# New places for a step's side work, an earlier head of the expert stage, and three of the last step's products with C on VectorE

## What is computed

```python
h = einsum('bhid,oi,od->bho', x, weighted_sum, weight)
x = layernorm(h)
for _ in range(4):
    xr = rmsnorm(x) @ W_in;  x_in, res = split(xr, 2)
    u = silu(causal_conv4(x_in) + conv_b)
    dt, Bm, Cm = split(u @ W_x)                       # 64, 16, 16
    delta = softplus(dt @ W_dt + b_dt)
    # for each of 16 states s, along the 512 tokens:
    h_s[t] = exp(delta[t] * A[s]) * h_s[t-1] + delta[t] * u[t] * Bm[t, s]
    y[t] = sum_s h_s[t] * Cm[t, s]
    x = ((y + u * Dp) * silu(res)) @ W_out
h = h + x
z = layernorm(h);  e = argmax(z @ W_router)
y = gelu(z @ W1[e] + b1[e]) @ Wo + bo + z             # per token, its own expert
out = h + layernorm(y) * gamma + beta
```

## Time and profile before

| | us |
|---|---|
| median of three runs (2059.36 to 2064.65) | 2062.27 |
| the profiled execution, and its span | 2073.18, 2071.5 |
| before the first scan | 141.4 |
| steps 0 to 13 | 1469.1 |
| step 14, step 15 | 94.5, 129.1 |
| after the last scan | 237.4 |

### The profile page before, as it was taken

How to read it: one execution, slowest core, us unless ns; L and a number is a source line. 1 busy time by engine, 2 the same in 40 slices (tenths; PEclk the granted TensorE clock), 3 DMA queues, 4 the chain that set the end, 5 groups by cost and what they waited for, 6 DMA issues and landing times.

```text
span 2071.5 us, 31985 instructions
## 1 busy us (share of the span) xinstructions
PE 1850.7 (89%) x12240; PEld 1465.2 (71%) x12240; DVE 1564.5 (76%) x1703; ACT 1464.7 (71%) x2467; POOL 1538.3 (74%) x896
## 2 busy tenths in 40 slices
PE   6989899999999999999999999999898986779994
PEld 3447677777777777777777777777677775669893
DVE  1358989798989897979798988888888887752232
ACT  0268888888888888888878787878797884613231
POOL 0039898889898988888888888888989896750331
PEclk9989999999999999999999999999999998899997
DMA  7211111111111111110111111111111112152542
GB/s 248 101 51 43 52 43 61 43 62 43 62 43 62 43 61 43 48 55 34 62 41 63 41 63 42 63 41 63 42 63 41 53 52 72 62 178 85 226 144 91
DMA packets 46394, 144.27 MB, mean 70 GB/s; under 512 B 7009, under 2 KB 18529, under 8 KB 42914
## 3 DMA queue, kind: packets, MB, share of 16 engines
...
## 4 chain that ended last, share of the span: by engine, by line
PE 52%; DVE 19%; issue 12%; ACT 12%; POOL 2%; DMA 2%; SPq 0%; DVEq 0%; POOLq 0%; ACTq 0%
PE b_ps L1316 12%; DVE hid L1043 10%; PE y_all L1327 9%; ACT dub_t L694 6%; ACT hid L681 5%; DVE u L851 4%; PE bank_b L1199 3%; PE bank_a L1449 3%; PE y_all L1118 3%; PE bank_b L1214 3%; PE bank_a L1223 3%; PE b_ps L1434 2%; PE y_all L1434 2%; PE bank_a L1247 2%; PE bank_a L1214 2%
## 5 line engine op out<-in xcount | busy, mean ns | idle before, releaser
L1043 DVE TENSOR_TENSOR_SCAN hid<-hid,b_ps 128x512 f32<-128x512 f32 x1024 | 1218.3, 1210 | 243.2 <-PE b_ps L1316 222.8
L504 POOL TENSOR_TENSOR hid<-hid,c_rep 128x1024 f32<-128x1024 f32 x512 | 1210.3, 2383 | 221.5 <-DVE hid L1043 221.5
L1316 PEld LDWEIGHTS b_ps<-ident,dub_t 128*128 128x128 f32 x4096 | 488.7, 143 | 375.5 <-issue 231.1
L1316 PE MATMUL b_ps<-ident,dub_t 128*128 128x128 f32 x4096 | 634.9, 278 | 78.9 <-DVE hid L1043 74.9
L681 ACT ACTIVATE hid<-delta,neg_a 128x512 f32<-128x512 f32 x1024 | 652.7, 710 | 0.2
L1327 PE MATMUL y_all<-ident,hid 128*128 128x128 f32 x4096 | 620.6, 275 | 3.8 <-POOL hid L504 3.8
L694 ACT ACTIVATE dub_t<-du_t,b_t 128x512 f32<-128x512 f32 x768 | 490.2, 711 | 54.8 <-PE b_ps L1316 53.1
L1327 PEld LDWEIGHTS y_all<-ident,hid 128*128 128x128 f32 x4096 | 485.7, 143 | 4.8 <-POOL hid L504 4.8
L495 POOL TENSOR_SCALAR dub_t<-du_t,b_t 128x512 f32<-128x512 f32 x256 | 173.8, 707 | 0.0
L1199 PE MATMUL bank_b<-xn,w_in_sb 128*128 128x512 f32 x256 | 134.5, 612 | 15.6 <-DVE xn L838 12.5
L851 DVE SCALAR_TENSOR_TENSOR u<-bank_b,conv_w_sb,u 128x511 f32<-128x511 f32 (+2 forms) x192 | 139.4, 726 | 0.7
...
## 6 DMA issues: line engine op xcount, KB each, us to landing
c_rep<-bc_dram SPq DMA_DIRECT2D x128, 512.0 KB, 3.6
...
```

Source lines behind the costliest of these rows:

```text
L504: nc.gpsimd.tensor_tensor(part, part, c_rep[:, n % 2, s % GROUP, :].unsqueeze(1) .broadcast_to([P, HALF, SEQ]), ALU.mult).then_inc(hc_read ...
L1043: nc.vector.tensor_tensor_scan(hid[:, i % RING, d, :], hid[:, i % RING, d, :], b_ps[d % 2][:, :], 0.0, ALU.mult, ALU.add)\
L1316: last = nc.tensor.transpose(b_ps[d % 2][:, c * P:(c + 1) * P], dub_t[:, i % DUB, c, d * P:(d + 1) * P], ident[:, :])
```

## The change

**Places in a step.** All tables have new places, and a piece of one step may now stand in the next one's first places ((16, 0) is place (0, 0) of the next step), so that `LATE_TAP_AT` and `LATE_OUT_AT` go. Each piece waits for what last used its bank, by a function for each kind (`x_bank_free`, `r_bank_free`, ...). `squares` and `mean_square` go to `bank_b`. `b_turn` is four full transposes instead of four products with 16 columns. ScalarE's side work stands in `between(k, s, part)`: before the decays, in the middle of them, behind them, in the middle of the products with B, behind these. There are four table loads in state 4 instead of two in a step. `POOL_B` is (4, 7, 9, 13), and GpSimd's `times_u` and `root` stand half a state later.

**Step 14 and 15.** Batch 0's `h_turn`, `join`, moments and scaling move to step 14 with their loads, batch 1's to earlier places in step 15, `rank(0)` and `lay_out(0)` to states 10 and 11. In step 15 ScalarE makes the products with B of all states, and VectorE multiplies states 13 to 15 with C (`last_times_c`, six instructions). GpSimd loads the weights of tiles 0 to 2 and sends z within step 15.

**Experts.** `tile_turn(0)` and `expert(0)` stand directly behind the last sums; `last_back`, `last_out`, `h_turn(2)` and the routing of batches 2 and 3 between the first seven tiles. A turn (`TURNS`) no longer spans both halves: tiles 10 and 21 are turned alone. GpSimd loads the weights up to tile 11 before it sends the second half.

```diff
+TURNS = [tuple(range(t, min(t + 2, TILES))) for t in range(0, TILES, 2)]
+TURNS += [tuple(t + TILES for t in turn) for turn in TURNS]
...
-POOL_B = (6, 7, 10, 12)
+DVE_C = 13
+POOL_B = (4, 7, 9, 13)
...
+            def act_b(k):
+                return tuple(range(STATE)) if k == STEPS - 1 else ACT_B
...
+                            if k == STEPS - 2 and g == 4:
+                                load_h(0)
+                                load_x_tokens(0)
...
+                    LOAD_W1_AT = {(11, 1): 0, (14, 0): 1, (15, 0): 2}
+                    SEND_Z_AT = {(12, 0): (0, 1), (12, 1): (2, 3), (13, 0): (4, 5), (13, 1): (6, 7)}
...
+                                if inner(k) or (live(k) and s < DVE_C):
                                     times_c(k, s, half)
-                                if live(k + 1) and (s, half) == (6, 1):
+                                if live(k + 1) and (s, half) == (7, 0):
                                     times_u(k + 1, 0)
-                                if live(k + 1) and (s, half) == (7, 1):
+                                if live(k + 1) and (s, half) == (8, 0):
                                     times_u(k + 1, 1)
...
+                    def between(k, s, part):
+                        at = (s, part)
...
+                        if at == (4, 1) and live(k + 1):
+                            nc.scalar.preload_act_table(ACT.Silu)
+                            gate(k + 1, 1)
+                            gate(k + 1, 0)
+                            for m in range(NI):
+                                silu(k + 1, m)
+                            nc.scalar.preload_act_table_set("natural_log_exp_and_others")
+                        if at == (4, 3) and live(k + 1):
+                            nc.scalar.preload_act_table(ACT.Silu)
+                            gate(k + 1, 2)
+                            gate(k + 1, 3)
+                            nc.scalar.preload_act_table_set("natural_log_exp_and_others")
...
+                    def last_times_c(s, half):
+                        k = STEPS - 1
...
+                        dve.wait_ge(scanned, NI * (STATE * k + s) + HALF * (half + 1))
+                        part = hid[:, (STATE * k + s) % RING, half * HALF:(half + 1) * HALF, :]
+                        nc.vector.tensor_tensor(part, part, c_rep[:, n % 2, s % GROUP, :].unsqueeze(1)
+                                                .broadcast_to([P, HALF, SEQ]), ALU.mult).then_inc(hc_last, 1)
...
-                    SOFTPLUS_AT = {(7, 0): 0, (7, 1): 1, (8, 0): 2, (8, 1): 3}
+                    SOFTPLUS_AT = {0: (6, 3), 1: (7, 2), 2: (8, 0), 3: (8, 1)}
...
-                    MOMENTS_AT = {(2, 3): 0, (10, 1): 1}
-                    SCALE_AT = {(4, 2): 0, (11, 3): 1}
+                    MOMENTS_AT = {(STEPS - 2, 11, 0): 0, (STEPS - 1, 5, 3): 1}
+                    SCALE_AT = {(STEPS - 2, 13, 0): 0, (STEPS - 1, 7, 0): 1}
...
-                            last = nc.tensor.matmul(bank_b[:, c * STATE:(c + 1) * STATE], dbl[:, c * P:(c + 1) * P],
-                                                    ident[:, RANK:RANK + STATE], start=True, stop=True)
+                            last = nc.tensor.transpose(bank_b[:, c * P:(c + 1) * P], dbl[:, c * P:(c + 1) * P], ident[:, :])
...
-                    DUT_AT = {(9, 2): 0, (10, 1): 1, (11, 0): 2, (11, 2): 3}
-                    BACK_AT = {(4, 2): 0, (5, 1): 1, (8, 0): 2, (8, 3): 3}
+                    DUT_AT = {0: (10, 0), 1: (10, 1), 2: (10, 2), 3: (11, 2)}
+                    BACK_AT = {0: (4, 3), 1: (6, 0), 2: (8, 3), 3: (9, 0)}
+                    SQUARES_AT, B_TURN_AT, SPREAD_AT = (6, 0), (6, 3), (8, 3)
```

More of the change, by code:

```diff
@@ L1102, in _ @@
                             finish(1)
-                        if t % 2:
-                            keep_y(t // 2)
+                        if t in (turn[-1] for turn in TURNS):
+                            keep_y(TURN_OF[t])
                     tail_moments(2)
@@ new lines, in _ @@
+                                for piece, place in OUT_AT.items():
+                                    if inner(k - 1) and place == at:
+                                        out_x(k - 1, *piece)
+                                if (k, s, d) in H_TURN_AT:
+                                    h_turn(*H_TURN_AT[k, s, d])
+                                if (k, s, d) in Z_TURN_AT:
+                                    z_turn(*Z_TURN_AT[k, s, d])
+                                if (k, s, d) in LOGITS_AT:
+                                    logits(LOGITS_AT[k, s, d])
```

696 lines of the change are left out of this document (403 added, 293 removed), and 6 rows, old and new, of the table TAP_AT.

## The result

The changed kernel takes **1891.9 us** (median of four runs, 1891.3 to 1892.6) against 2062.2 for the one before: a ratio of 0.9175, with a 95% interval of 0.9159 to 0.9191. Forecast were 1913, between 1885 and 1972. The profiled execution has a span of 1889.3 us.

What follows compares the result with a forecast made beforehand. No engine alone accounts for the 104.4 us step, TensorE comes nearest. Steps 0 to 13 -112, step 14 +3.5, step 15 -22.5, the rest -18.5: -149.5 off 2062.3 gives 1913 us, range 1885 to 1972.

Steps and rivals of the forecast that it cites:

- The account of the old step: Old middle step: TensorE work 93.7 us, stretches at VectorE's pace 6.4, named waits 3.8; 103.9 against 104.4 measured.
- Alignment: Old step: five stretches run at VectorE's pace where its pieces stand closer than TensorE's, costing 6.4 us.
- named waits: Old step: TensorE waits 3.8 us at back(2), spread_norm, in_x and to_delta; costed at 0 in the new step.
- 94.9 for the new step: New middle step: TensorE work 93.4 us, 1.0 for two stretches at VectorE's pace, and the 0.5 left over.
- the 0.5 left over: Old step: the part of the measured 104.4 us that the account's 103.9 does not explain.
- The 97 taken for the step: Steps 0 to 13: 97 us a step, 96 for step 0, with three engines between 90 and 95.7; -112 us.
- rival D: Steps: account right, slack of 1.5 us not needed, 95.6 a step, 1893 us; chance 0.65 together with the forecast.
- Rival A: Steps: only the named waits go, waits for scans move elsewhere, 100.5 us a step, 1963 in all; chance 0.20.
- Step 14: Step 14 takes over batch 0's head, 8 us of VectorE partly beside GpSimd's work; 94.5 becomes 98, +3.5 us.
- Step 15: Step 15: VectorE busy 101.5 us plus 5 of idle time, 106.5 instead of 129.1; -22.5 us.
- the prediction's own sign, under 110 us: Step 15 was to take under 110 us without a TensorE wait for a DMA.
- Behind the last scan: After the last scan: first expert 5.5 us behind it (-26), moved work +12, waits and half clock -4.5; sum -18.5.

Runs made afterwards that it cites:

- poolb_old: Changed kernel with the states whose B products GpSimd makes put back from 4, 7, 9, 13 to 6, 7, 10, 12: 1959.9 us, ratio 0.9468.
- shifts_only: Changed kernel with step 15's routings, ranks and layout one place later and first z sends behind GpSimd's second product of state 12: 1885.8 us, ratio 0.9149.

## Why the prediction was right, and where it was not

**The account of the old step: right.** Alignment and named waits were put as separate terms of 6.4 and 3.8 us a step. At full clock the runs give 3.5 for the taps alone and 2.5 for the early `back` and `spread_norm`, and both together bring back 6.2 to 6.4 of the 9.5; the other 3.2 no run tests. The account's 94.9 for the new step is what was measured, with the 0.5 left over carried from the old step; what that 0.5 is stays open.

The pattern step left one thing out. Five of the old steps 1 to 13 take 106.1 to 106.4 us, the other eight 104.4 to 104.8, and each of the five has one stretch of half clock. No wait stands ahead of it: in the 6 us before it TensorE is busy without a gap, with `squares` (L1180, 16 products of one column) and the old `b_turn` (L1234, eight products of 16 columns). Step 5, whose clock stays up, and step 6 (L1316, L1327 and L1247 as in the earlier trace rows):

```profile
698.03 1.84 PE L1180 MATMUL bank_a<-ones,xn 128*128 128x1 f32 x16
...
700.64 0.96 PE L1234 MATMUL bank_b<-ident,dbl 128*128 128x16 f32 x8
701.45 0.64 PE L1316 MATMUL b_ps<-ident,dub_t 128*128 128x128 f32 x4
...
805.04 0.96 PE L1234 MATMUL bank_b<-ident,dbl 128*128 128x16 f32 x8
805.86 0.84 PE L1316 MATMUL b_ps<-ident,dub_t 128*128 128x128 f32 x4
806.49 1.06 PE L1327 MATMUL y_all<-ident,hid 128*128 128x128 f32 x4
807.34 1.92 PE L1247 MATMUL bank_a<-dbl,w_dt_sb 128*128 128x512 f32 x2
```

No trace of the changed kernel or its variants has half clock at this place in steps 1 to 13. There `b_turn` is full transposes and stands three places behind `squares` instead of one. So the turn, priced at 0.36 us a step, may have brought some 9 us more over the steps; no run puts it or `squares` back, so this is not shown.

**The 97 taken for the step: the term that was mis-sized.** "With three engines between 90 and 95.7 us I take 97" added 2.1 us a step to the account, and rival D was right that this slack is not needed: 0.3 us of waits for GpSimd a step, not 0.8, and no wait for ScalarE. That is 31 us of the total. poolb_old shows that the margin is one of places and not of busy time: with the work of each engine unchanged, ScalarE's copies come late and cost 3.9 us a step. Rival A (100.5) did not come; the waits for scans did not move elsewhere, they fell to 6.2 us in fourteen steps.

**Step 14: the size was off by 2 us, the mechanism was missing.** The moments were priced by their sum in the old trace, 2.3 us. In the new place one of them is held for 5.2 us, 0.9 more goes on the scaling, and TensorE then ran on at half clock.

**Step 15: busy time right, idle time wrong.** Forecast were 101.5 busy and 5 idle; it was 100.65 and 13.8, and the prediction's own sign, under 110 us, was missed. Five of the six products took 1.23 us (1.14 from start to start), the first 3.49. In that busy time are 10.5 us in which six instructions were held by GpSimd, and behind each TensorE waits for a scan (2.2 to 3.8 us, 17.5 of the 22.4 us of such waits in the step), which then comes back as VectorE's idle time. The old step 15 had as much: its 98.0 busy hold 10.9 us in which 14 instructions were held, and TensorE's waits for scans were 19.4. The forecast carried the held time over unseen inside the 98.0, so its busy time is right in part by luck, and it took nearly all idle time away, while only the waits for the DMA (9.6) and most of that for ScalarE (3.6 to 0.9) went. In shifts_only, with 4.2 us less of holds, VectorE is busy for 4.5 us less and idle for 1.7 us less. The Trainium skill's rule (SBUF — State Buffer, Who interferes with whom) was weighed for the six products alone, where it decided 2.3 us. It agrees with these traces on the other held pieces: each has two inputs in SBUF or is a TENSOR_SCALAR from SBUF to SBUF, and the statistics and the scans beside them are not held.

**Behind the last scan: right.** The first expert starts 5.4 us behind the last scan (5.5), the end takes 29.1. From the first expert to the last `keep_y` it is 179.2 us, 3.4 more than before and not 7.5: half of the old waits and half clock was given back in the forecast, and nearly all went. TensorE of the changed kernel at the first expert, and the last `keep_y` (compare):

```profile
1680.95 3.84 PE L1571 MATMUL b_ps<-hid,delta 128*128 128x128 f32 x32 [0.78 <-DVE hid L1069]
...
1860.19 0.42 DVE L1077 COPY hid<-bank_a 128x256 f32<-128x256 f32 x1 [3.81 <-PE bank_a L1587]
```

**The prologue** was left at 0 and gave 6.5: TensorE's granted clock there was 0.99 instead of 0.94. In the other traces of kernels with this prologue it takes 135.3 to 137.6 us, so that part of it is the single execution.

**The rest of the sum.** The misses are -31 for the steps and -2 for all else; +12 goes the other way, because 11 us of the old profiled execution were no part of the median but were taken off both. Together 21, which is 1913 against 1892. Two errors cancel in part here, and that is luck. It is luck too that rival D's 1893 meets 1892 so closely: its steps were 11 us short of the measured gain, and these same 12 us made up for it.
